# Where zeroes, masks and residual shift rows are made in a two-layer graph network kernel

## The reference

```
layer 0: x = sum of
           gat(8 heads x 128, then 1 head x 768)(norm(x))   # softmax over the edges of a node, + bias b2
           mlp( ln2( norm(x) + performer(norm(x), M=384) @ W_proj + b_proj ) ) + residual
         then a routed expert feed-forward
layer 1: x = gat(8 heads x 96, then 1 head)(xn) + b2                     # "gnn_b2"
           + x2 + gamma * ln( xn + performer(xn, M=256) @ W_proj + b_proj ) + beta
         then a feed-forward with ternary weights
ln(z)  = (z - mean(z)) / sqrt(var(z) + 1e-5)
```

## Time and profile before

| what | value |
|---|---|
| median of 3 runs | 3404.73 us (3403.36 to 3406.1) |
| profiled execution | 3403.53 us |
| its span in the trace | 3401.4 us |
| mean granted clock of TensorE | 0.93 |
| PE, PEld, DVE busy in the span | 84%, 74%, 69% |
| ACT, POOL busy | 43%, 16% |
| DMA: q1, q0 | 29.8%, 6.5% of 16 engines' span |

### The profile page before, as it was taken

One profiled execution on the slowest core, in us unless ns is written; L12 is line 12 of the kernel. 1 busy time (PEld: TensorE's weight loads), 2 busy tenths in 40 slices (PEclk: granted clock), 3 DMA queues, 4 the chain that ended last, 5 costly groups with the idle time before them and its releaser, 6 DMA issues. The chain is left out here.

```text
span 3401.4 us, 50787 instructions
## 1 busy us (share of the span) xinstructions
PE 2869.5 (84%) x17896; PEld 2528.3 (74%) x17896; DVE 2332.3 (69%) x4168; ACT 1460.6 (43%) x2436; POOL 530.0 (16%) x358
## 2 busy tenths in 40 slices
PE   1999997877999997887997599878999977887795
PEld 1999996766888997777896233247999977777794
DVE  4765642856842544998664888657788868998775
ACT  3464652222112332554243577521556522554345
POOL 2677783220000000000002300000000022000000
PEclk9999998988999998999998699979999988998897
DMA  8433326684213554523131311253311068213301
GB/s 263 84 51 57 47 22 155 215 206 111 67 44 87 174 165 118 140 67 84 29 75 48 80 42 43 55 165 119 77 41 51 23 174 224 76 46 79 85 21 47
DMA packets 254534, 319.48 MB, mean 94 GB/s; under 512 B 98467, under 2 KB 176804, under 8 KB 254206
## 3 DMA queue, kind: packets, MB, share of 16 engines
q1 hardware_dynamic: 176574, 272.11, 29.8%
q0 software_dynamic: 77760, 44.83, 6.5%
HBM read 236.35 MB, written 79.53 MB: 93 GB/s over the span
## 5 line engine op out<-in xcount | busy, mean ns | idle before, releaser
L210 POOL DMA_INDIRECT adj_d<-edge_val,edge_off x160 | 336.3, 2102 | 150.8 <-DMA adj_d<-edge_val,edge_off 59.2
L3274 DVE TENSOR_TENSOR expert_wgel<-expert_gel,expert_wps 128x417 f32<-128x417 f32 (+1 forms) x384 | 202.8, 584 | 57.0 <-PE expert_wps L3199 47.3
L2185 PE MATMUL gat00att_ops<-gat00att_h,gat00att_p 125*125 x1600 | 198.8, 280 | 50.4 <-DVE gat00att_p L2159 50.4
L2185 PE MATMUL gat10att_ops<-gat10att_h,gat10att_p 125*125 x1600 | 195.9, 279 | 47.1 <-DVE gat10att_p L2159 47.1
L2185 PEld LDWEIGHTS gat00att_ops<-gat00att_h,gat00att_p 125*125 125x125 f32 x1600 | 184.7, 190 | 64.6 <-issue 64.5
L2185 PEld LDWEIGHTS gat10att_ops<-gat10att_h,gat10att_p 125*125 125x125 f32 x1600 | 184.0, 192 | 59.1 <-issue 59.1
L3246 ACT ACTIVATE expert_gel<-expert_hps 128x417 f32<-128x417 f32 (+1 forms) x384 | 193.8, 519 | 63.7 <-DVE expert_wgel L3274 52.3
L596 PE MATMUL perf_wide<-y_lo,perf_qk_hi 128*128 128x416 f32 (+1 forms) x432 | 155.5, 360 | 44.6 <-DVE perf_qk_lo L780 44.0
L734 ACT ACTIVATE xn_room<-perf_wide,perf_lnm 125x384 f32<-125x384 f32 (+2 forms) x228 | 114.2, 622 | 158.5 <-PE perf_wide L620 85.6
L1358 PE MATMUL fc_ps<-y_lo,fc_w_hi 128*128 128x512 f32 (+1 forms) x432 | 154.6, 358 | 21.4 <-DVE fc_w_lo L1400 21.4
L1511 PE MATMUL fc_ops<-fc_w_hi,fc_x_lo 128*125 128x384 f32 x480 | 163.7, 341 | 7.1 <-DVE fc_w_lo L1563 7.1
(11 more groups left out here) (503 smaller groups left out, 8281.1 us busy)
## 6 DMA issues: line engine op xcount, KB each, us to landing
fc_w<-in_L_mix_fc_w SPq DMA_DIRECT2D x96, 384.0 KB
adj_d<-edge_zero POOLq DMA_DIRECT2D x22, 546.9 KB, 28.0
gat00proj_adj<-adj_d POOLq DMA_DIRECT2D x20, 546.9 KB, 8.2
edge_keys<-keys_d SPq DMA_DIRECT2D x20, 437.5 KB
gat00att_sh<-shift_d SPq DMA_DIRECT2D x16, 546.9 KB
sh<-shift_d SPq DMA_DIRECT2D x16, 546.9 KB
perf_w<-in_L_mix_qkv_w SPq DMA_DIRECT2D x18, 384.0 KB
perf_w<-in_L_mix_W_qkv SPq DMA_DIRECT2D x18, 384.0 KB
```

The source lines that it names most:

```text
L210: edges.nc.gpsimd.indirect_dma_start(out=edges.adj_flat[u].rearrange("(n a) -> n a", a=1), out_offset=bass.IndirectOffsetOnAxis(ap=edges.o ...
L2185: ins = pe.matmul(ops[0:TP, u, b, t * w:(t + 1) * w], p[:, s, (t0 + t) * TP:(t0 + t + 1) * TP], h[:, s, bass.ds(hd, 1), :], start=(s == 0 ...
L3274: dve.tensor_tensor(wgel[:, q % W, 0:cn], gel[:, q % 3, 0:cn], wps[:, q % 3, 0:cn], ALU.mult).then_inc(wgel_done, 1)
```

## The change

It has five parts.

1. The norm stage zeroes only the first adjacency matrix. The other is zeroed by GpSimd at the start of `EdgeCounts.add`, in perf0.
2. gat00proj takes its 20 half tiles of counts by a table `due` with 2 or 3 for each tile from 1, so that none is left behind the loop. Before, three were behind the last product.
3. proj_stage has no GpSimd block. DVE adds the bias itself (`base`), ACT normalises with scale and bias columns (`normalise`), DVE makes these columns (`scales`) and the sums (`total`). a(1) is loaded ahead of the weights. DVE waits for the bias, in proj1 also for gamma, ahead of its tile loop.
4. proj1 loads neither beta nor b2 and adds no shift.
5. In perf1 GpSimd adds beta, and later b2, to all rows of x2 in DRAM by accumulating DMAs: two for beta behind the loads of mask and row 0, two for b2 behind the load of row 3. x2 is written in mix and next read in proj1.

```
-    def clear(self, pool):
-        for flat in self.adj_flat:
+    def clear(self, pool, flats):
+        for flat in flats:
...
     def add(self, pool):
         edges, added, sets = self.edges, self.added, len(self.edges.adj_flat)
+        edges.clear(pool, edges.adj_flat[1:])
         pool.wait_ge(edges.cleared, edges.cleared_n)
...
-                edges.clear(pool)
+                edges.clear(pool, edges.adj_flat[0:1])
...   performer_stage, GpSimd, with scan
-                    scan.load(pool)
+                    def add_row(hd):
+                        if hd not in (1, 4):
+                            return
+                        if hd == 4:
+                            pool.wait_ge(row_added, 32)
+                        for r0, r1 in ((0, ROWS), (ROWS, TP)):
+                            row = row_bcast(shifted[1][hd // 4], r1 - r0).unsqueeze(1).to_broadcast([r1 - r0, NT, D])
+                            pool.dma_start(tokens(shifted[0])[r0:r1], row, accum_op=ALU.add).then_inc(row_added, 16)
+
+                    scan.load(pool, add_row)
+                    pool.wait_ge(row_added, 64)
...   MaxScan.load
         for hd in range(self.heads):
             u = hd % self.slots
+            if beside is not None:
+                beside(hd)
...   proj_stage, SP
                 load_a(0)
+                load_a(1)
                 for kb in range(KB):
                     load_w(kb)
-                load_a(1)
...
-                        move_rows(sp, rows[0:TP, k, :], row_bcast(r, TP), rows_ld)
-                if more is not None:
-                    move_rows(sp, more[:], row_bcast(more_shift_d, TP), rows_ld)
+                else:
+                    move_rows(sp, rows[:], row_bcast(gain, TP), rows_ld)
...   proj_stage, ACT (called behind root; the GpSimd block is gone)
+                def normalise(t):
+                    act.wait_ge(centred, t + 1)
+                    act.activation(a[:, t, :] if turn else h[:, t, :], h[:, t, :], ACT.Identity, scale=rstd[:, t:t + 1],
+                                   bias=centre[:, t:t + 1]).then_inc(normed, 1)
...   proj_stage, DVE
+                def base(t):
+                    if t in first_of:
+                        dve.wait_ge(xn_ld[first_of[t]], 32)
+                    steps_done.done(dve.tensor_tensor(h[:, t, :], h[:, t, :], bias[:], ALU.add))
...
+                def scales(t):
                     dve.wait_ge(std_ready, t + 1)
                     steps_done.done(dve.reciprocal(rstd[:, t:t + 1], std[:, t:t + 1]))
                     steps_done.wait()
+                    dve.scalar_tensor_tensor(out=centre[:, t:t + 1], in0=mv[:, t, 0:1], scalar=-1.0, in1=rstd[:, t:t + 1],
+                                             op0=ALU.mult, op1=ALU.mult).then_inc(centred, 1)
...
+                dve.wait_ge(bias_ld, 32)
+                if not turn:
+                    dve.wait_ge(rows_ld, 32)
                 for t in range(NT):
                     if t + 1 < NT:
                         low_a(t + 1)
+                    if t:
+                        scales(t - 1)
+                    base(t)
                     project(t)
                     if t:
-                        normalise(t - 1)
+                        total(t - 1)
...   gat_project_stage
+        due, halves = [[]], iter(range(2 * NT))
+        for t in range(1, NT):
+            due.append([next(halves) for _ in range(3 if t in (4, 7) else 2)])
...   gat_project_stage, PE, in the tile loop; c is the half of the product
-                            turn_counts(2 * t - 2 + c)
+                            for q in (due[t][1:] if c else due[t][0:1]):
+                                turn_counts(q)
                 if edges is not None:
-                    turn_counts(2 * NT - 2)
-                    turn_counts(2 * NT - 1)
```

More of the change, by code:

```diff
@@ L1006, in __init__, with proj_stage @@
         self.tiles, self.stored = tiles, nc.alloc_semaphore(f"{name}_late_st")
-def proj_stage(nc, name, ident, attn_d, w_d, bias_d, xn_d, x_d, sum_d, eps, gain, shift, yT, ahead=(), more_shift_d=None,
+def proj_stage(nc, name, ident, attn_d, w_d, bias_d, xn_d, x_d, sum_d, eps, gain, shift, yT, ahead=(),
                shift_of=None, first=None, late=None):
@@ L1036, in proj_stage @@
         bias = S.sb("bias", [TP, D])
-        rows = S.sb("rows", [128, 2, KB if turn else D])
-        more = S.sb("more", [TP, D]) if more_shift_d is not None else None
+        rows = S.sb("rows", [128, 2, KB]) if turn else S.sb("gain", [TP, D])
         stats = S.sb("stats", [TP, NT, 2, 6])
@@ L1041, in proj_stage @@
         std = S.sb("std", [TP, NT])
-        rstd = S.sb("rstd", [TP, NT])
+        rstd, centre = S.sb("rstd", [TP, NT]), S.sb("centre", [TP, NT])
         epst = S.sb("epst", [TP, 1])
@@ L1198, in _ @@
                         root(t - 1)
+                        normalise(t - 1)
                     if turn and t >= 3:
@@ L1201, in _ @@
                 root(NT - 1)
+                normalise(NT - 1)
                 if turn:
@@ L1204, in _ @@
                         keep_y(t)
[L1206 to L1209, removed]
-                        pool.wait_ge(xn_ld[first_of[t]], 32)
-                    pool.tensor_tensor(h[:, t, :], h[:, t, :], bias[:], ALU.add).then_inc(based, 1)
-                def shift_row(t):
-                    if t in first_of:
-                        pool.wait_ge(x_ld[first_of[t]], 32)
-                    pool.tensor_tensor(x[:, t, :], x[:, t, :], rows[0:TP, 1, :], ALU.add).then_inc(shifted, 1)
-                pool.wait_ge(bias_ld, 32)
-                base(0)
-                base(1)
-                if not turn:
-                    pool.wait_ge(rows_ld, 96 if more is not None else 64)
-                    if more is not None:
-                        pool.tensor_tensor(rows[0:TP, 1, :], rows[0:TP, 1, :], more[:], ALU.add).then_inc(more_added, 1)
-                        pool.wait_ge(more_added, 1)
-                    shift_row(0)
-                    shift_row(1)
-                for t in range(2, NT):
-                    base(t)
-                    if not turn:
-                        shift_row(t)
             @block.vector
@@ L1291, in _ @@
                         low_a(t + 1)
+                    if t:
+                        scales(t - 1)
+                    base(t)
                     project(t)
-                    if t == 0 and not turn:
-                        dve.wait_ge(rows_ld, 96 if more is not None else 64)
                     if t:
-                        normalise(t - 1)
+                        total(t - 1)
                     if turn and t >= 4:
                         split_y(t - 4)
-                normalise(NT - 1)
+                scales(NT - 1)
+                total(NT - 1)
                 if turn:
@@ L1627, in gat_project_stage @@
             turns += [("x", t + 1)] if t + 1 < NT else []
-            turns += [("m", 2 * t - 2), ("m", 2 * t - 1)] if edges is not None else []
-        turns += [("m", 2 * NT - 2), ("m", 2 * NT - 1)] if edges is not None else []
+            turns += [("m", q) for q in due[t]] if edges is not None else []
         nth = {turn: n for n, turn in enumerate(turns)}
@@ L1925, in _ @@
                         low(t)
-                    if edges is not None and t >= 2:
-                        keep_mask(2 * t - 4)
+                    if edges is not None and pending:
+                        keep_mask(pending.pop(0))
                     if t >= 2:
```

61 lines of the change are left out of this document (30 added, 31 removed).

## The result

The changed kernel takes 3418.42 us (median of 6, 3416.35 to 3423.55), the kernel before 3402.51 in the same comparison; the ratio is 1.0054 with a 95% interval of 1.0043 to 1.0065. It is slower, by 15.9 us between the medians and some 18 by the ratio, more than the 0.2% that can be told from no change, and inside the range of 3381 to 3429. It is not the case that I held likeliest, 3405 with gain and loss nearly even. The time lies where rival C, the slow accumulating row, put it.

The account below looks back on a forecast made before the run. PE was taken to bound perf0 and perf1, waits for loads and DVE the projections, DMA norm. Terms −17.5 + 1.1 − 5 − 6.8 and +30 for perf1 sum to +1.8: 3405 us, range 3381 to 3429.

Parts of the forecast that it names:

- the case that I held likeliest: Rows in perf1 at 0.24 to 0.33 us, perf1 costs 21 to 35 and eats the gain: 3396 to 3411; chance 0.38.
- rival C: perf1: accumulating rows at 0.36 to 0.46 us, DVE's two weight splits wait, costing 37 to 53: 3412 to 3429; chance 0.28.
- Part 1, zeroes: norm gains 21.1 us, the second matrix's zeroes delay perf0; together they gain 17.5 (bounds 10 and 21).
- the 2 us for the delayed v weights: perf0: zeroes delay the v weights by 2 us, so PE's own work would end at 530.
- Part 2, masks: gat00proj: five transposes moved ahead of the last output tile delay its store; cost 1.1 us (−1 to +3).
- Part 3, the projections: Without GpSimd's additions beside DVE, proj0 gains 5 us (3.7 to 6) and proj1 6.8 (5 to 9).
- spares nothing at first: proj0: loading tile 1 ahead of the weights gains nothing at first, as the weights' last block sets the first product.
- Part 4, perf1: perf1: accumulating rows delay DVE's two splits of v weights, +17 and +13 us, costing 30 in all.
- the price T of a row: perf1: DMA engine time per accumulating 3072 B row, taken as 0.30 us, bounds 0.13 and 0.46.
- my formula for the first meeting: perf1: 58 weight packets per engine each alternate with one row, 58 × (0.04 + T); weights land 14.5 us late.
- the second meeting: perf1: the add behind row 3 meets the next v weights; 16 us late, some 3 vanish in later waits: +13.
- The rule of the Trainium skill: perf1: engines take whole packets per queue, so weights come nearly as early; perf1 loses 2 us, 3377; rival E, chance 0.07.

Follow-up runs that it names:

- e8: Changed kernel with tile 1 of the attention output loaded behind the weights again in proj0 and proj1; ratio to before 1.0063, proj0 103.1 us.
- e6: Changed kernel with DVE's waits for bias and gamma moved later, to behind low_a(1) and ahead of total(0); ratio to before 1.0050, proj1 91.1 us against 96.2.
- e3: Changed kernel with perf1's four DMAs writing the same rows to a scratch tensor instead of adding; ratio to before 1.0019, 3406 us, perf1 408.5 us.

## Why the prediction was right or wrong

**Part 1, zeroes.** Right, within 2.5 us: 15.0 gained where I had 17.5. norm ended near 63 and GpSimd's first add waited for the zeroes, as forecast. The cost in perf0 was forecast as the chain's, with PE's own work ending at 530 and the stage at 531.6. It was PE's: it waited 6.78 us (1.5 before) for v weights that the zeroes delayed, 5 us and not 2, and the chain ended 2.6 us ahead of PE's last store. The term that was mis-sized is the 2 us for the delayed v weights, which were 5. "Ends 435.9 us after it begins" came out at 433.1 here, but the chain's length is no constant.

**Part 2, masks.** Wrong: +8.6 where I had +1.1 (−1 to +3). The step counted the transposes, five by 0.6 us, and where they stand in PE's order. It didn't ask what each waits for one place earlier. The rows for it were there, in the windows of the kernel before (columns as in the earlier trace rows):

```profile
609.10:629.10 20.00, 20.00 (x105) 16.63 (x104) 17.33 (x17) 5.81 (x9) 6.29 (x12) 1.00 0.91 297
```

PE is busy without a gap and DVE for 17.3 of 20 us, so a request made earlier to DVE had little room.

**Part 3, the projections.** The sign and the rough size are right; that GpSimd's absence is what gained is read from the durations below, no run puts its block back. GpSimd's hindrance is gone, as forecast. The product with gamma in the lines by form of DVE in proj1, whose mean was 1718 ns:

```profile
L1270 DVE TENSOR_TENSOR proj_h<-proj_h,proj_gain 125x768 f32<-125x768 f32 x10 | 9.1, 912 | 1.1 <-ACT proj_h L1176 1.1
```

In proj0 the gain was 8.4 instead of 5, since I held that the early tile 1 "spares nothing at first", the weights setting the first product. PE's timeline of the kernel before says otherwise:

```profile
705.26 1.51 PE L1129 MATMUL proj_tps<-ident,proj_a 125*128 125x125 f32 x6 [9.68 <-DMA proj_a<-attn_d]
```

That is tile 1, turned in front of the first product, and PE waited 9.68 us for its load. e8 gives some 3 us for the edit. In proj1 the wait for gamma was forecast with its place and its victim, and cost somewhat more than I gave it: 5 us by e6, where I had 2.7.

**Part 4, perf1.** The mechanism was right, place by place: the adds stand behind the mask and behind row 3, take turns with SP's packets one by one, and DVE's splits of v weights wait. Two sizes were off. The first is the price T of a row, for which I took 0.30 us. Its mean was 0.32 in the first add, inside my 0.24 to 0.33, and 0.37 in the second, above it. The second is the step from the price to the wait. With 0.324 my formula for the first meeting gives 58 × 0.364 = 21.1 us and a landing at 2415.1, 15.9 late; it was 19.9 late, measured from the start of each stage (44.2 against 24.3). The queues of the changed kernel from the same place in the stage, 19.1 us in, to the split of the v weights (2377.3 to 2402.4):

```profile
q0 software_dynamic: 1148, 3.38, 90.5%
q1 hardware_dynamic: 1123, 0.59, 12.8%
```

A turn took 25.1 × 16 / 1123 = 0.36 us in the mean of the 16 engines, as in the formula. But DVE waits for the last weights of the last engine, and for its 58 turns (62 by the 987 packets of 512 B in this window) that engine would have needed 0.40 to 0.43 us each. That is an estimate; no view tells the engines apart. For the second meeting the formula gives 21.1 late with 0.365, and the split came 24.5 later as seen from the load of row 3. There I took 3 us off for waits behind it that would shrink, and they gave nothing back.

So perf1's 15 us over the forecast are some 6.5 for the price (1.4 and 5.1), 7.4 for waits longer than the mean turn gives (4.0 and 3.4) and 3 that were not given back, less some 2: beyond the two delays the stage lost 0.9 us, where I had 2 to 3 for the cold clock.

What is a row's price made of? The quickest took 0.252 us, where the quickest plain row took 0.12 and where the earlier trace rows give 0.13. That fits two passes over the row, as in my own reading (two reads with the write beside them, 0.26 at 0.13 a pass), and not three (0.39). What drives the mean up to 0.32 and 0.40 is the slow packets, and e3 has those with no adding. What makes them slow these runs don't tell. A sign of them was in the earlier trace rows: 0.854 × 12 × 16 / 498 = 0.33 us for a packet of 4.6 KB, where the plain rate of the earlier trace rows gives 0.19.

**The rule of the Trainium skill** (page "DMA: Bandwidth & Descriptors", section "Queues, rings and completion order"), that an engine drains a whole packet of some 9 to 17 descriptors from one queue before it goes to the next, would have made perf1 lose 2 us. If what the profile counts is the descriptor, no run here agrees with it: 498 to 605, 241 to 243, 297 to 285, at the most two for one in e3, and 45 us lost.

**The sum.** 1.8 was forecast, 19.5 measured in the span: 15 of the difference are perf1's, 7.5 the masks', 2.5 norm's and perf0's, −5.5 the projections', and −2 the stages' that the change leaves alone. Rival C gave 3412 to 3429 and had the place and the time, but its price, 0.36 to 0.46, holds only for the second add and for adds that run alone, and its reason only in part: the quickest rows cost two passes, not three. That the time lies inside my range is owed in part to its width, and to errors of the masks and the projections that went against each other. What would have moved me towards C is to price the wait by the last engine instead of the mean one, and the row by the slow packets of the earlier trace rows.

## What to carry to other kernels

Work that is moved to a queue nobody seems to use is not free. Here two queues of the same DMA engines took turns packet by packet, so a long list of dear packets held back every small one issued beside or behind it; ask who asks for its next input in that stretch, and place the list where nobody does. Price the wait by the engine that is last, not by the mean. Here the same 2500 rows cost 45 us at two places and nothing at two others. When a step is moved earlier in an engine's order, look up what it waits for; when a load is moved, read which wait really ends last ahead of the first product.

## What the runs showed of the hardware

- An accumulating DMA of 3072 B rows from DRAM into DRAM: the quickest row took 0.252 us of a DMA engine's time in every add (two passes at the quickest plain row's 0.12), the mean was 0.32 and 0.37 beside SP's loads and 0.39 to 0.40 alone.
- A plain copy of the same rows went in packets of two rows: 0.234 us a packet where quickest, 0.41 and 0.51 in the mean. So part of the rows are slow with and without adding; why is not shown.
- Rows of half the size took 0.139 us where quickest, 0.20 and 0.24 in the mean.
- While the adds were in full run, the software queue and SP's queue alternated one to one with rows of 3072 B (242 to 241, 241 to 243) and of 1536 B (380 to 374, 297 to 285); with plain packets of 6144 B first one to one (354 to 353), then 163 to 337.
- GpSimd's chain of 160 indirect adds took from 423.6 to 435.9 us in the same code in different kernels, and 429.2 and 429.3 in two profiles of one kernel; what shortens it is not settled.
